# First tile of a cross network gathered by field and placed by TensorE, second tile's partners awaited in two parts

## The reference

```python
x0 = inputs; xk = inputs
for W in filters:                       # (39*39,128), (128*39,128), (128*39,128)
    z = jnp.einsum('bfd,bgd->bfgd', x0, xk).reshape(b, f * g, d)
    cur = jnp.einsum('bpd,pm->bmd', z, W)
    outs.append(cur); xk = cur
z = jnp.sum(jnp.concatenate(outs, axis=1), axis=-1)      # (1024, 384)
h = relu(concat([z, dense_ctx]) @ W_top1 + b_top1)
h = relu(h @ W_top2 + b_top2)
y = h @ W_top3
```

## Time and profile before

| | |
|---|---|
| median of three executions | 1282.8 us |
| the profiled execution, time | 1282.42 us |
| its span | 1280.6 us |
| PE busy in the span | 1243.7 us (97%) |
| DVE, ACT, POOL busy | 1052.2, 952.7, 955.7 us (82%, 74%, 75%) |

### The profile page before, as it was taken

The page is one execution under the profiler, slowest core; times in us unless marked ns, Lnnn a source line. Parts: engine busy times, 40 slices in busy tenths (PEclk is TensorE's granted clock), DMA queues, the critical chain, the costliest instruction groups (busy, mean ns, idle before and its releaser), DMA issues. The chain is left out here.

```text
span 1280.6 us, 21991 instructions
## 1 busy us (share of the span) xinstructions
PE 1243.7 (97%) x5919; PEld 1010.2 (79%) x5919; DVE 1052.2 (82%) x3208; ACT 952.7 (74%) x3115; POOL 955.7 (75%) x743
## 2 busy tenths in 40 slices
PE   3699999999999999999999999999999999999998
PEld 2477778888788887888878888788878888888887
DVE  3499999788987899788897799978899788988873
ACT  2488888678876788678886788867888678877772
POOL 7588888678886888767886778867888678874461
PEclk9899999999999999999999999999999999999999
DMA  6474334331333332323333133332233332232000
GB/s 154 106 208 84 79 82 82 80 69 44 69 74 79 80 71 58 71 53 83 82 78 74 29 70 83 83 79 56 45 73 79 81 80 59 59 67 67 4 1 1
DMA packets 137182, 92.02 MB, mean 72 GB/s; under 512 B 92355, under 2 KB 100035, under 8 KB 136718
## 3 DMA queue, kind: packets, MB, share of 16 engines
q1 hardware_dynamic: 126819, 87.99, 30.0%
q0 software_dynamic: 10240, 2.64, 2.6%
HBM read 84.08 MB, written 3.87 MB: 69 GB/s over the span
## 5 line engine op out<-in xcount | busy, mean ns | idle before, releaser
L423 ACT ACTIVATE parts<-pieces,x_cols 128x128 f32<-128x128 f32 x2560 | 728.1, 373 | 236.1 <-PE pieces L746 179.5
L571 DVE SCALAR_TENSOR_TENSOR parts<-pieces,x_cols,parts 128x128 f32<-128x128 f32 x2432 | 685.5, 345 | 180.6 <-PE pieces L746 133.5
L744 PE MATMUL pieces<-w_hi,cur_hi 128*128 128x512 f32 (+1 forms) x1280 | 543.0, 424 | 9.8 <-issue 6.2
L746 PE MATMUL pieces<-w_hi,cur_lo 128*128 128x512 f32 (+1 forms) x1280 | 498.7, 390 | 0.0
L745 PE MATMUL pieces<-w_lo,cur_hi 128*128 128x512 f32 (+1 forms) x1280 | 498.6, 390 | 0.0
L372 POOL TENSOR_TENSOR parts<-parts 128x1024 f32<-128x1024 f32 x127 | 304.7, 2400 | 184.9 <-DVE parts L571 180.2
L363 POOL DMA_INDIRECT emb<-in_table,rows x320 | 312.6, 977 | 81.9 <-issue 67.3
L744 PEld LDWEIGHTS pieces<-w_hi,cur_hi 128*128 128x128 f32 x1280 | 241.7, 189 | 68.4 <-issue 10.7
L746 PEld LDWEIGHTS pieces<-w_hi,cur_lo 128*128 128x128 f32 x1280 | 241.0, 188 | 51.8
L745 PEld LDWEIGHTS pieces<-w_lo,cur_hi 128*128 128x128 f32 x1280 | 241.9, 189 | 50.7
L377 POOL TENSOR_TENSOR tails<-parts 128x512 f32<-128x512 f32 x127 | 164.3, 1294 | 18.1
(11 more groups left out here) (81 smaller groups left out, 633.6 us busy)
## 6 DMA issues: line engine op xcount, KB each, us to landing
partners<-x_wide SPq DMA_DIRECT2D x93, 468.0 KB
x_end<-x_wide SPq DMA_DIRECT2D x96, 80.0 KB
x_rep<-x_wide SPq DMA_DIRECT2D x96, 78.0 KB
partners<-x_wide SPq DMA_DIRECT2D x93, 80.0 KB
emb<-in_table,rows POOLq DMA_INDIRECT x320
x_diag<-x_cols SPq DMA_DIRECT2D x256, 10.0 KB
partners<-x_wide SPq DMA_DIRECT2D x31, 132.0 KB
x_wide<-emb SPq DMA_DIRECT2D x32, 80.0 KB
```

What stands on the lines that cost most here:

```text
L423: last = nc.scalar.activation(parts[n % 2][:, 4 * i + r, :], src[:, r * H:(r + 1) * H], ACT.Copy, scale=x_cols[n // 4][:, n % 4, f:f + 1])
L571: nc.vector.scalar_tensor_tensor(acc, src[:, r * H:(r + 1) * H], x_cols[n // 4][:, n % 4, f:f + 1], acc, ALU.mult, ALU.add).then_inc(acc_d ...
L744: nc.tensor.matmul(dst[:, 0:width], hi[:, cols], w1_hi[:, ws], start=True, stop=False)
L746: nc.tensor.matmul(dst[:, 0:width], lo[:, cols], w1_hi[:, ws], start=False, stop=True).then_inc(l2d_ready if q in D_PIECES else l2a_ready, 1)
```

## The change

The first tile is gathered apart. Partition r\*39+f holds field f of examples 11r to 11r+10, so that 11 gathers of 117 useful rows bring it. Six small matmuls with 0/1 matrices (`place_rows`) put it three times over the partitions in a PSUM bank, and ACT copies it to `x_rep`. The first tile's `x_end` comes from an eighth shift matmul (`shift_end`) and a copy on ACT. Nothing of the first tile is stored to memory.

The w1 split is made in three steps, not two. For every tile `partners` is loaded in two parts, slices 0 to 2 (`partners_loaded`) and 3 to 6 (`partners_late`), with `x_end` between them; DVE waits for the first part before k = 0 and for the second before k = 3 (`LATE`). The second tile's pairs stand at steps 8, 12, ... (`S_BEGIN`) where they stood at 3, 7, ...; their sums follow 5 steps later, where it was 7.

On POOL the two clearings of `x_diag`, the last gather of the third tile and the addition for the fourth tile's rows move behind the first block's tree. On SP `x_diag` of the first tile is loaded behind all loads of the third tile.

```diff
-WARM_UP = 14
+WARM_UP = 10
...
+        self.pair = [begin + 4 * k for k in range(PAIRK)]
+        self.high = [x + 1 for x in self.pair]
+        self.low = [x + 2 for x in self.pair]
+        self.sum = [x + lag for x in self.pair]
+        self.x_bank = begin - 2
+        self.x_end = self.pair[FULL - 1] + 2
+        self.cur1 = self.sum[-1] + 1
...
+LATE = PAIRK // 2
+S_USUAL, S_BEGIN = Steps(3, 7), Steps(8, 5)
+FIRST_OF_TWO = 9
...
+FIRST = -(-TILE_B // REP)
+FIRST_EARLY = 8
...
+            sp.dma_start(ids_first[:], t["ids_first"]).then_inc(ids_first_loaded, 16)
+            sp.dma_start(take_low[:], t["take_low"]).then_inc(take_low_loaded, 16)
...
+            sp.dma_start(place_rows[0:REP * F], t["place_rows"]).then_inc(place_loaded, 16)
+            sp.dma_start(shift_rows[0:F], t["shift_rows"]).then_inc(shift_loaded, 16)
...
-            store_tile(0, 0)
-            load_x(0, 0)
             store_tile(1, 1)
             load_x(1, 1)
             sp.wait_ge(w0_lo_ready, 1)
-            load_partners(1, 1)
-            sp.wait_ge(diag_cleared, 2)
-            load_diag(0, 0)
+            load_partners(1, 1, 0, LATE, partners_loaded)
+            load_late(1, 1)
...
-                        load_partners(tile + 2, (i + 2) % TILES)
+                        load_partners(tile + 2, (i + 2) % TILES, 0, LATE, partners_loaded)
+                        load_late(tile + 2, (i + 2) % TILES)
+                    if first and i == 0:
+                        sp.wait_ge(diag_cleared, 2)
+                        load_diag(0, 0)
...
+            def gather_first():
+
+                pool.wait_ge(ids_first_loaded, 16)
+                pool.tensor_tensor(rows_first[:], ids_first[:, 0, :], ids_first[:, 1, :], ALU.add).then_inc(rows_ready, 1)
+                pool.wait_ge(rows_ready, 1)
+                for j in range(FIRST):
+                    pool.indirect_dma_start(
+                        emb_first[:, j, :], None, t["table"],
+                        bass.IndirectOffsetOnAxis(ap=rows_first[:, j:j + 1], axis=0)
+                    ).then_inc(first_gathered[0 if j < FIRST_EARLY else 1], 16)
...
+                    if first and n == 0:
+                        add_parts(u, n)
+                        for j in range(FIRST_OF_TWO, GATHERS):
+                            gather(2, 2, j)
+                        find_rows(3, 3)
+                    if first and n in (1, 2):
+                        pool.memset(x_diag[n - 1][:], 0.0).then_inc(diag_cleared, 1)
...
+            act.wait_ge(x_first_made, 1)
+            nc.scalar.activation(x_rep[0][:], x_first[:], ACT.Copy).then_inc(x_first_ready, 1)
...
+                if k == 2:
+                    act.wait_ge(x_end_first_made, 1)
+                    nc.scalar.activation(x_end[0][:], x_end_first[0:LAST_ROWS, :], ACT.Copy
+                                         ).then_inc(x_end_first_ready, 1)
...
-                    dve.wait_ge(partners_loaded[i % 2],
-                                (tile - i % 2) * 8 * PARTNER_LOADS + i % 2 * 16 * PARTNER_LOADS)
+                    dve.wait_ge(partners_loaded[i % 2], (tile + i % 2) * 8 * PARTNER_LOADS)
+                if k == LATE:
+                    dve.wait_ge(partners_late[i % 2], (tile + i % 2) * 8 * LATE_LOADS)
...
-            dve.wait_ge(const_loaded, 3 * 16)
+            dve.wait_ge(take_low_loaded, 16)
             dve.wait_ge(w0_hi_ready, 1)
...
+            def place_first(early):
+
+                pe.wait_ge(first_gathered[early], 16 * (FIRST_EARLY if early == 0 else FIRST - FIRST_EARLY))
+                for r in range(REP):
+                    a, b = (0, FIRST_EARLY) if early == 0 else (FIRST_EARLY, min(FIRST, TILE_B - r * FIRST))
+                    last = nc.tensor.matmul(x_first[:, (r * FIRST + a) * D:(r * FIRST + b) * D],
+                                            place_rows[0:REP * F, r, :],
+                                            emb_first[0:REP * F, a:b, :].rearrange("p g d -> p (g d)"),
+                                            start=True, stop=True)
...
             pe.wait_ge(w1_hi_ready, 1)
-            pe.wait_ge(gathered[0], GATHERS * 16)
             warm_up(WARM_UP, pieces[0])
-            pe.wait_ge(const_loaded, 3 * 16)
+            pe.wait_ge(place_loaded, 16)
+            place_first(0)
+            place_first(1)
+            pe.wait_ge(shift_loaded, 2 * 16)
             for k in range(PAIRK):
                 shift_first(k)
                 if k == 1:
                     transpose_x(0, 0, 0)
+            shift_end()
```

More of the change, by code:

```diff
@@ L52, with __init__ @@
 PARTS = 4 * len(A_PIECES)
-WARM_UP = 14
+WARM_UP = 10
 TREE = 3
 BANKS = 4
[L59 to L64, removed]
+class Steps:
+    def __init__(self, begin, lag):
+        self.pair = [begin + 4 * k for k in range(PAIRK)]
[7 more added lines that the diff above has]
+S_USUAL, S_BEGIN = Steps(3, 7), Steps(8, 5)
 S_X = 17
+FIRST_OF_TWO = 9
 G_LAG = 3
@@ L201, in cin_kernel @@
         partners_loaded = [sem(f"partners_loaded{i}") for i in range(2)]
+        partners_late = [sem(f"partners_late{i}") for i in range(2)]
         pairs_ready = sem("pairs_ready")
@@ L228, in cin_kernel @@
         out_stored = sem("out_stored")
+        half = F - PARTS
+        w1_steps = [(w1_raw[0][0], w1_raw[0][1], w1_loaded[0])] + [
+            (parts[1][:, a:b, :], slice((PARTS + a) * H, (PARTS + b) * H), w1_loaded[1])
+            for a, b in ((0, half // 2), (half // 2, half))]
         block = ctx.enter_context(nc.Block())
@@ L403, in quad @@
                         find_rows(tile + 1, i + 4)
-                    if not (last and n == BLOCKS - 1):
+                    if not (last and n == BLOCKS - 1) and not (first and n == 0):
                         add_parts(u, n)
@@ L542, in quad @@
                                 copy_y(u - 1)
-                        if more and s == S_SUM[-1] + 1:
+                        if more and s == steps.cur1:
                             copy_cur1_hi(tile + 1, i + 1)
@@ L674, in quad @@
                                 step(u - 1, BLOCKS + n - 2)
-                        if more and s in S_PAIR:
-                            make_pairs(tile + 1, i + 1, S_PAIR.index(s))
-                        if more and s in S_LOW:
-                            take_pairs_low(tile + 1, i + 1, S_LOW.index(s))
-                        if more and s == S_SUM[-1] + 2:
+                        steps = S_BEGIN if first and i == 0 else S_USUAL
+                        if more and s in steps.pair:
+                            make_pairs(tile + 1, i + 1, steps.pair.index(s))
+                        if more and s in steps.low:
+                            take_pairs_low(tile + 1, i + 1, steps.low.index(s))
+                        if more and s == steps.cur1 + 1:
                             take_cur1(tile + 1, (tile + 1) * TILE_B, i + 1)
@@ L841, in quad @@
                             transpose_x(tile + 1, (i + 1) % TILES, g_made(u, at))
-                        if more and s in S_SUM:
-                            sum_pairs(tile + 1, i + 1, S_SUM.index(s))
+                        steps = S_BEGIN if first and i == 0 else S_USUAL
+                        if more and s in steps.sum:
+                            sum_pairs(tile + 1, i + 1, steps.sum.index(s))
                         if at in G_STEP:
```

137 lines of the change are left out of this document (86 added, 51 removed).

## The result

The changed kernel takes **1289.42 us** (median of 6 runs, 1288.51 to 1291.51), the kernel before took 1282.39 beside it (6 runs): ratio 1.0057, interval 1.0045 to 1.0069. It is 7 us slower where 6.4 faster was forecast. The profiled execution took 1291.51 us, the longest of the six; its span is 1289.7, 9.1 more than that of the kernel before.

What follows compares the result with a forecast made beforehand. PE, 97% busy, was taken as the bound, with time lost only at the start. Block 0's end at 49.9 plus 29.1 put the second tile at 79.0 against 85.44: 1282.4 - 6.4 = 1276.0, 1276.4 as median; range 1272.5 to 1282.6.

Steps and rivals of the forecast that it cites:

- The shifts start at 24.5, against 24.70: First tile on PE: dropping the store and reload, less added gathers, placing and copy, starts the shifts 0.2 us earlier.
- Fourth, one shift more: First tile on PE: an eighth shift matmul, at 0.86 us each, delays the sums; first layer 2 piece at 41.5.
- rival B: First tile's shifts run at half clock after PE idles about 3.6 us; costs 1.7 us, gain 4.7, 1278.1; chance 0.16.
- Without the first two waits DVE would have stood at that pair product: Block 0: the second tile's partners, all there at 56.51, bound the PE hole even without ACT's and DVE's "remote" waits.
- The hole goes: Block 0: with partners in two waits and later pairs, DVE ends at 49.9 instead of 61.24, 11.3 us won there.
- C: Block 0: "remote" waits stay, perhaps from full DMA engines, freeing ACT and DVE only at 55.1; 1287.7 us; chance 0.10.
- In one line: gain = 85.44 - (last DVE operation of block 0 + 29.1).: Block 0's end to the second tile, with POOL's longer list: second tile at 79.0 against 85.44, 6.4 us earlier.
- the gap between the trees: POOL between first and second tree: a 5.2 us tree, then 9.2 us of six gathers, a clearing and a row addition.
- the last two tail additions: DVE in block 3, ahead of `cur1_lo` and the second tile: two tail additions taking 0.65 us.
- DVE's last operation of block 0 ends 8.4 us after the first piece: Block 0 on DVE: PE's 6.7 us, a pair product of 0.6 and DVE's own lag, ending at 49.9.

Runs made afterwards that it cites:

- e1: The changed kernel with its shift matmuls zero-padded to contract over 128 rows, not 39: 1288.52 us (1.0047).
- e2: The changed kernel, 39-row shifts kept, with 9 more warm-up matmuls between the early and late placing and 3 behind the late one: 1288.97 us (1.0049).
- r9: The kernel before, unchanged, measured again in a later session: 1281.36 us.
- e5: The changed kernel with shifts over 128 rows and POOL's list of before, late pair steps kept: 1274.48 us (0.9938).
- e6: e5 with the usual pair steps (3, lag 7) for the first tile too: 1272.12 us (0.9920).
- r16: e6 measured again, as control of the last session: 1273.42 us (0.9926).
- e4: The kernel before with only partners in two waits, pairs at later steps and the first tile's `x_diag` loaded later: 1281.69 us (0.9995).
- r14: e5 with SP's partner loads for the second tile held until DVE has weighed two pieces of block 0, in a later session: 1282.39 us (0.9997).
- e3: The changed kernel, 39-row shifts, with clearing, ten third-tile gathers and both row additions ahead of block 0's tree again: 1285.79 us (1.0029).
- e8: e5 with the third tile's ten gathers and their row addition moved behind block 0's tree: 1283.41 us.
- r10: The changed kernel measured again in a later session: 1291.30 us.
- r11: e3 measured again in a later session: 1287.36 us.
- r12: e5 measured again one session later: 1281.58 us.
- r17: e6 with the last row addition and two gathers of POOL's series moved behind block 0's tree: 1273.07 us (0.9924).
- r18: e6 with the clearing cut into eight pieces that stand between the third tile's ten gathers: 1274.01 us (0.9929).
- r15: e8 measured again in a later session: 1286.6 us (1.0038).
- r13: e6 measured again in a later session: 1281.06 us (0.9986).

## Why the prediction was wrong

*"The shifts start at 24.5, against 24.70"*. Right within a microsecond: 23.69, and 21.7 to 23.7 in the kernels with this start. The stretched gathers are there (3.51 and 1.85 us), and the gain at this point was 1.0 for a forecast 0.2.

*"Fourth, one shift more. Seven with the transposes took 24.70 to 30.95, 0.86 each"*, and from it the first piece at 41.5. **The first step that failed**, with rival B beside it. I costed eight shifts by rows of 128-row matmuls and never priced that the new ones take 39 of them. B knew the half clock but sized it at 1.7 us, a cold start that activity would end. It lasted 20.5 us: from first shift to first sum 14.45 us, where the working had 7.15 (6.25 of the earlier trace rows, and 0.9). The first piece came at 54.20, 12.7 us behind the 41.5: 7.3 of that are the shifts. e1 and e2 show the rows as cause.

*"Without the first two waits DVE would have stood at that pair product, so the partners bound this hole either way ... The hole goes."* The first half stands: r9 waits 2.12 us more for the partners behind the hold, in the sessions without the hold their last part lands at 56 to 58 us, and there the kernel before stays at 1282.3 and 1282.5 while e5, e6 and r16 take 1272 to 1274.5. **The second step that failed** is *"The hole goes"*: it took the two "remote" waits for harmless, but they are a bound of their own. e4 takes the partners' wait away and gains nothing (0.9995), r14 has the hold with no partner load in flight. C named this hold, with 0.10, and gave it a fixed end at 55.1 and the full DMA engines as reason. Both were wrong: its place goes by POOL's gathers. The change itself drew it forward. With the clearing taken from ahead of them the third tile's gathers began at 33.71 instead of 36.48, and the hold met the sums, which the slow shifts had put there (from 43.5 us on, and from 40.9 in e1; e3, with the old list, has it in block 0 from 45.2). That C's 1287.7 lies near the measured 1289.42 is luck: block 0 ended late by way of the shifts and the sums too. That is why 7.4 us won in e1 at the first sum came out as 0.9 in the medians, within the noise: a stage that ends earlier only waits longer for the same release.

*"In one line: gain = 85.44 - (last DVE operation of block 0 + 29.1)."* Right as a sum: 63.30 + 29.4, and the trees are 13.8 apart where 5.2 + 9.2 = 14.4 were forecast. Two parts of it were off and nearly cancel: the gap between the trees was 0.6 less, and the last two tail additions took 2.2 us for the 0.65 of both. e3 with the old list has 26.5 us in place of 29.4; half of these 2.9 us is ACT's later start at block 3 (19.15 us behind block 0's end, against 17.71), half the tail additions. The term was called what remains once the hole is gone; with the hole still there it is a plain loss, part of the 3.6 us between e3 and the changed kernel. What it left out is the 1.6 us that the clock costs behind the 3.77 us wait.

*"DVE's last operation of block 0 ends 8.4 us after the first piece"*. Right where no hold is: 8.36 in e5, 8.59 in e8, 9.1 in the changed kernel.

The account at the second tile, 7.26 us late: block 0 ends 2.06 later (late sums and hold, less the shorter block 0), 2.9 are POOL's list (29.4 less e3's 26.5; between the copies r10 and r11 only 1.4), and 2.3 are what e3 and e4 (26.5, 26.6) have over the kernel before (24.2), perhaps the pairs at later steps. That these are the cause is not shown, nor that they cost time at the end of the run: e5 has 26.2 and e6, with the usual steps, 25.9, and in time e5 against e6, and e4 against before, tell nothing apart.

Luck had a part in the good numbers: e5 and r12 are one kernel, and its 1274.48, near the forecast 1276.4, came from a session without the hold, while 1281.58 came from one with it.

**What stays open.** It is open why the hold is absent in two sessions (seven kernels: 1272 to 1284 us) and present in all the other traces, among them copies of e5 to e8, for e5 even on the same chip. The kernel before has medians of 1281.7 to 1282.8 in either kind of session; it was traced only where the hold was, so whether it had the hold in the others is not known. Through what a series of gathers holds TensorE's signals no run shows, nor whether the recording of the trace takes part, nor whether fewer or sparser gathers would end it (r17 and r18 met a session without it).

## What to carry to other kernels

A matmul's cost at another clock is part of the cost of a new operation: before a stage is moved to TensorE, see whether any row has that shape at the full clock, and pad the contraction to 128 rows where the tile is there anyway. A wait that the profile cannot name ("remote") is a bound of its own: earlier work ahead of it is swallowed. A wait that stands right behind it in the trace is a second bound, and taking either away alone gains nothing or little. Work that an engine did in its free time at the start (here POOL's clearing and gathers) is not free any more once it stands behind the first block's tree.

## What the runs showed of the hardware

- TensorE's clock fell from 1.00 to 0.50 (2.4 to 1.2 GHz) amid gapless 39-row fp32 matmuls, and came back only 5.4 us after those over 128 rows had begun (e2: half from 26.86 to 40.51, sums from 35.08, PE busy 5.00 of 5.00 us in both rows from 26 to 36). The same matmuls padded to 128 rows took the clock up (e1, full from 26.12).
- After a wait of 3.77 us without a matmul the clock fell to 0.50 again, 0.9 us behind the first matmul (changed kernel, 92.70), and cost 1.6 us; after waits of 2.1 to 2.4 us it fell in some traces (r11, r14) and not in others (e3, r12).
- In some sessions a long series of gathers on POOL goes with waits of 3 to 11 us in ACT and DVE for matmuls that had long been executed; in the changed kernel, e1 and e2 three partner issues of SP then take 2.8 us instead of 1.2. It moved with the gathers (r15), and needs no other DMA traffic to speak of (r14: 16 GB/s). In these sessions, and only in them, records of semaphore updates within 2 us of a gather are missing.
- A gather issued while DVE splits w1 takes 3.51 us instead of 0.94 (changed kernel, 14.44); a tail addition of DVE beside POOL's tree takes 1.23 us (changed kernel) instead of 0.33 (e3).
- One kernel can differ by 0.6 to 0.7% between two sessions (e5 1274.48, r12 1281.58 in one run; e6 1272.12, r13 1281.06), with the spread within a session at 0.2 to 0.4%.
